# An attention and MLP kernel on one core: the value products of two half groups put into one run, numerators in two PSUM banks in turn, denominators in a projection bank, and the end of the program rearranged

## What is computed

```python
q = ((seq2 + b_self) @ Wq + bq)          # split into 16 heads of 32
k1 = ((x + b_prev) @ Wk + bk); k2 = ((seq2 + b_self) @ Wk + bk)
v1 = x @ Wv + bv;              v2 = seq2 @ Wv + bv
score = concat(where(mask, q @ k1.T, -inf), sum(q * k2)) * SCALE
w = softmax(score)
x = x + (w[:-1] @ v1 + w[-1] * v2) @ Wo + bo
h = gelu(x @ W1 + b1)                     # 2048 wide
x = x + concat(h @ W2 + b2, h @ We[e] + be[e])
```

## Time and profile before

| | us |
|---|---|
| median of 3 runs | 1795.75 (1795.39 to 1795.79) |
| profiled execution | 1807.21 |
| its span, first to last instruction | 1805.1 |
| PE busy | 1719.9 (95%) |
| mean granted PE clock | 0.976 |

### The profile page before, as it was taken

The page is one execution under the profiler, slowest core; times in us unless marked ns, Lnnn a source line. Parts: engine busy times, 40 slices in busy tenths (PEclk is TensorE's granted clock), DMA queues, the critical chain, the costliest instruction groups (busy, mean ns, idle before and its releaser), DMA issues.

```text
span 1805.1 us, 27962 instructions
## 1 busy us (share of the span) xinstructions
PE 1719.9 (95%) x8256; PEld 1262.1 (70%) x8256; DVE 942.4 (52%) x1430; ACT 709.5 (39%) x1259; POOL 663.4 (37%) x521
## 2 busy tenths in 40 slices
PE   6998999999999999999987899999999999999996
PEld 5765656666666666666652688888888888888885
DVE  4577576775866768757587643232232323232321
ACT  3253454444544445445344443323232323233222
POOL 3165577584874847748564301000010101010101
PEclk8999999999999999999996999999999999999998
DMA  6452444443534435244344342223131413232212
GB/s 143 76 114 51 91 103 107 86 97 73 120 90 91 96 85 119 69 103 87 80 110 121 109 122 50 68 48 86 46 87 41 87 52 75 61 66 72 47 30 53
DMA packets 370269, 149.45 MB, mean 83 GB/s; under 512 B 289226, under 2 KB 329162, under 8 KB 370194
## 3 DMA queue, kind: packets, MB, share of 16 engines
q1 hardware_dynamic: 364966, 146.28, 35.7%
q10 hardware_dynamic: 5228, 2.35, 0.5%
HBM read 70.41 MB, written 27.28 MB: 54 GB/s over the span
## 4 chain that ended last, share of the span: by engine, by line
PE 78%; issue 6%; DVE 5%; DMA 4%; SPq 3%; POOL 2%; ACT 1%; ACTq 0%; DVEq 0%; POOLq 0%
PE ps_proj L1258 14%; PE ps_max L1289 6%; PE ps_av L1210 6%; PE ps_av L1212 6%; PE ps_av L1211 6%; PE ps_av L1329 6%; PE ps_score L1316 5%; PE ps_proj L1210 3%; PE ps_proj L1211 3%; PE ps_proj L1212 3%; DMA stacks<-parts 3%; PE ps_score L1210 3%; PE ps_max L1212 3%; PE ps_score L1212 3%; PE ps_max L1210 3%
## 5 line engine op out<-in xcount | busy, mean ns | idle before, releaser
L729 ACT ACTIVATE p_f<-ps_score 128x512 f32<-128x512 f32 x512 | 303.8, 599 | 459.2 <-PE ps_score L1316 414.8
L941 DVE TENSOR_REDUCE m_col<-ps_max 128x1 f32<-128x512 f32 x512 | 328.7, 683 | 201.2 <-PE ps_max L1289 199.9
L604 POOL TENSOR_TENSOR p_sum<-p_sum,p_f 128x512 f32<-128x512 f32 x256 | 335.4, 1342 | 3.3 <-ACT p_f L729 3.3
L644 POOL TENSOR_TENSOR z_f<-z_f,a_raw 128x512 f32<-128x512 f32 x32 | 40.8, 1287 | 750.5 <-ACT z_f L842 730.0
L1135 DVE TENSOR_TENSOR h_lo<-h_f,h_hi 128x512 fp32r<-128x512 f32 x128 | 88.0, 687 | 412.2 <-ACT h_hi L833 412.1
L601 POOL TENSOR_TENSOR p_sum<-p_f 128x512 f32<-128x512 f32 x128 | 161.6, 1293 | 210.7 <-PE ps_av L1338 205.4
L1289 PE MATMUL ps_max<-stacks 97*128 97x512 f32 x512 | 189.3, 437 | 38.1 <-DVE m_col L941 19.4
L1258 PE MATMUL ps_proj<-in_hi,w_hi 128*128 128x512 f32 x512 | 207.8, 406 | 11.2 <-POOL in_lo L609 7.9
L1316 PE MATMUL ps_score<-stacks 99*128 99x512 f32 x512 | 209.0, 419 | 5.6 <-ACT p_f L729 5.4
L1210 PE MATMUL ps_av<-y_hi,w_hi 128*128 128x512 f32 x512 | 199.9, 390 | 6.6 <-ACT h_hi L833 3.8
L1258 PE MATMUL ps_proj<-in_lo,w_hi 128*128 128x512 f32 x512 | 205.6, 402 | 0.0
(11 more groups left out here) (122 smaller groups left out, 2729.1 us busy)
## 6 DMA issues: line engine op xcount, KB each, us to landing
stacks<-parts SPq DMA_DIRECT2D x384, 128.0 KB
raw<-in_x_dram SPq DMA_DIRECT2D x128, 64.0 KB, 2.3
raw<-in_fside_BxSxS_dram SPq DMA_DIRECT2D x128, 64.0 KB, 2.2
den<-own_scratch SPq DMA_DIRECT2D x128, 64.0 KB, 2.8
attn_scratch<-num SPq DMA_DIRECT2D x32, 256.0 KB, 3.0
x_raw<-in_x_dram SPq DMA_DIRECT2D x128, 64.0 KB, 2.2
we_raw<-in_L_cond_We_dram SPq DMA_DIRECT2D x32, 256.0 KB, 2.8
resid_scratch<-a_raw SPq DMA_DIRECT2D x32, 256.0 KB, 2.0
```

The costliest lines, as they stand in the source:

```text
L604: pool.tensor_tensor(p_sum[:, j], p_sum[:, j], now, ALU.add).then_inc(sum_made, 1)
L729: act.activation(p_f[:, i % FLIGHT], ps_score[i % 2][:, :], ACT.Exp, scale=SCALE).then_inc(p_made, 1)
L941: dve.tensor_reduce(m_col[:, n % C, n // C:n // C + 1], ps_max[n % 2][:, :], AX.X, ALU.max).then_inc(max_made, 1)
```

## The change

The batch's groups 1 to 3 do key tiles 2 and 3 of the group before in step 8, right ahead of tiles 0 and 1 of their own, so that 16 value products and 4 denominators stand in one run; group 0 keeps step 1. The numerators alternate between the two banks `ps_av`, the denominators go to `ps_proj[0]`, and DVE takes numerator and denominator together in step 10. The thirds of the projections are spread anew. In the last group the reciprocals and the normalization of the group before are put off until after the phase. In the MLP, `expert_high` of part 2 moves from slice 1 to slice 3 of the first batch. In the last batch the output products are reordered so that banks become complete one after the other, DVE adds bias and residual from PSUM and transposes, and SP and ACT store two quarters each; POOL, ACT and DRAM have no part in it.

```diff
@@ thirds_of
-            slots = ((4, 5, 5, 6, 7, 7, 9, 10, 11, 12, 13, 14), (0, 2, 3, 4, 5, 6, 9, 10, 11, 12, 13, 14),
-                     (0, 2, 3, 6, 7, 7, 9, 10, 11, 12, 13, 15), (0, 2, 3, 4, 5, 6, 9, 10, 11, 12, 13, 15))[g]
+            slots = ((4, 5, 5, 6, 7, 7, 9, 10, 12, 13, 14, 15), (0, 1, 3, 4, 6, 7, 9, 10, 12, 13, 14, 14),
+                     (0, 1, 3, 6, 7, 7, 9, 10, 12, 13, 14, 15), (0, 1, 3, 4, 6, 7, 9, 10, 12, 13, 14, 14))[g]
-        k_at, q_at = (6, 4, 4, 4), (8, 7, 8, 7)
+        k_at, q_at = (6, 4, 4, 4), (8, 8, 8, 8)
-        first_o = ps_proj + ps_max
+        first_o = (ps_proj[1], ps_max[0], ps_proj[0], ps_max[1])
-        ps_num, ps_den = ps_av
+        end_whole = (a_raw[:, 0], a_raw[:, 1], x_raw[:, :], x_t[:, :])
+        ps_den = ps_proj[0]
@@ ACT, rows
-                    if first and m < 2:
-                        expert_high(b, m + 1, True)
+                    if first and m in (0, 3):
+                        expert_high(b, 1 if m == 0 else 2, True)
@@ DVE, batch
-                        if i == 3 and started:
+                        if i == 10 and started:
                             numerator(*after(b, g, -1))
-                        if i == 10 and started:
                             denominator(*after(b, g, -1))
-                        if i in (13, 14) and started:
+                        if i in (13, 14) and started and not (last and g == C - 1):
-                        if i == 15 and started:
+                        if i == 15 and started and not (last and g == C - 1):
@@ DVE, new
+            def end_sum(c):
+                dve.wait_ge(end_mm, c + 1)
+                dve.wait_ge(whole_made, C * B)
+                if c == CS:
+                    dve.wait_ge(be_landed, DMA * B)
+                dve.scalar_tensor_tensor(out=end_z[:, c], in0=ps_out[c][:, :], scalar=bias_2[:, c:c + 1],
+                                         in1=end_whole[c], op0=ALU.add, op1=ALU.add).then_inc(end_made, 1)
+                dve.wait_ge(end_made, c + 1)
+                dve.transpose(end_z_t[:, c], end_z[:, c]).then_inc(z_t_made, 1)
@@ DVE, after the first phase
+            for n in range(4):
+                one_over_den(B - 1, C - 2, n)
+            normalize(B - 1, C - 2)
             hidden_low(0, 0)
@@ PE
                     if n == 2:
                         pe.wait_ge(q_hi_made, G + 1)
+                        wait(pe, den_made, G - 2)
-                    wait(pe, num_made, G)
+                    wait(pe, num_made, G - 1)
-                        if i == 1 and not (first and g == 0):
+                        if i == (8 if g else 1) and not (first and g == 0):
                             for t in (2, 3):
                                 value_burst(*after(b, g, -1), t)
                         if i == 8:
                             for t in (0, 1):
                                 value_burst(b, g, t)
                             if not (first and g == 0):
+                                if more:
+                                    pe.wait_ge(q_hi_made, C * b + g + 3)
+                                else:
+                                    pe.wait_ge(v2_made, C * B)
                                 denominators(*after(b, g, -1))
+            def end_outputs():
+                for m, c in ((KH - 2, 0), (KH - 2, 1), (KH - 1, 0), (KH - 1, 1),
+                             (KH - 2, 2), (KH - 1, 2), (KH - 2, 3), (KH - 1, 3)):
...
@@ SP and ACT, last batch
+            def end_result(c, quads):
+                sp.wait_ge(z_t_made, C * (B - 1) + c + 1)
+                for q in quads:
+                    sp.dma_start(blocks(out, B - 1, c, q),
+                                 end_z_t[QUAD * q:QUAD * (q + 1), c].rearrange("p (tb f) -> p tb f", f=QUAD)
+                                 ).then_inc(stored[c % 2], DMA)
```

More of the change, by code:

```diff
@@ L139, in cond_resid_program @@
         x_t = sb2("x_t", [P, S])
+        ending = two.enter_context(ExitStack())
+        end_z = ending.enter_context(nc.sbuf_tensor("end_z", [P, C, S], F32))
+        end_z_t = ending.enter_context(nc.sbuf_tensor("end_z_t", [P, C, S], F32))
+        ending.close()
         a_hi = sb2("a_hi", [P, C, S], F32R)
@@ L471, in batch @@
                         residual(0, 3)
-                    if not (first and g == 0):
+                    if not (first and g == 0) and not (last and g == C - 1):
                         store(*after(b, g, -1))
@@ L539, in rows @@
                     expert_weights(b, 3)
+                if last:
+                    for c in range(C):
+                        end_result(c, (0, 1))
+                    return
                 if not last:
@@ L646, in rows @@
             def rows(b, first, last):
-                for c in range(C):
+                for c in range(C if not last else 0):
                     add_residual(b, c)
@@ L878, in rows @@
                         y_high(b + 1, c)
-                for c in range(C if last else 2):
-                    result(b, c)
+                    for c in range(2):
+                        result(b, c)
+                else:
+                    for c in range(C):
+                        end_result(c, (2, 3))
             batches(act, rows)
@@ L1175, in rows @@
                         w2_low(w2_row[m])
-                    if first and m < 2:
-                        expert_low(b, m + 1)
+                    if first and m in (0, 3):
+                        expert_low(b, 1 if m == 0 else 2)
                     if m == (6 if first else 4):
@@ L1186, in rows @@
                     if 3 + C <= m < 3 + 2 * C:
-                        whole(b, m - 3 - C)
+                        if last:
+                            end_whole_of(m - 3 - C)
+                        else:
+                            whole(b, m - 3 - C)
                     if not last and m == KH - 4:
@@ L1200, in rows @@
                         y_low(b + 1, c)
-                for c in range(C if last else 2):
-                    turn_result(b, c)
+                for c in range(C):
+                    if last:
+                        end_sum(c)
+                    elif c < 2:
+                        turn_result(b, c)
             batches(dve, rows)
@@ L1448, in outputs @@
                 mm.then_inc(out_mm, 1)
+            def end_outputs():
+                for m, c in ((KH - 2, 0), (KH - 2, 1), (KH - 1, 0), (KH - 1, 1),
+                             (KH - 2, 2), (KH - 1, 2), (KH - 2, 3), (KH - 1, 3)):
+                    if c == 0:
+                        pe.wait_ge(h_lo_made, KH * (B - 1) + m + 1)
+                    at = slice(P * c, P * (c + 1))
+                    left = (w2_hi[:, m, at], w2_lo[:, m, at]) if c < CS else (we_hi[:, m], we_lo[:, m])
+                    mm = three(ps_out[c][:, :], left, (h_hi[:, m % 2], h_lo[:, m % 2]), False, m == KH - 1)
+                    if m == KH - 1:
+                        mm.then_inc(end_mm, 1)
             def rows(b, first, last):
@@ L1463, in rows @@
                         hidden(b, m + 2, range(C), first)
+                    if last and m == KH - 2:
+                        end_outputs()
+                        break
                     outputs(b, m, first)
```

25 lines of the change are left out of this document (19 added, 6 removed).

## The result

Measured: 1815.42 us (median of 6 runs, 1807.8 to 1837.05), against 1795.57 us before (6 runs, 1791.86 to 1796.51), ratio 1.0097 with a 95% interval of 1.0076 to 1.0119. Ratios leave out a run that lies more than 1.5% above the fastest of its kernel, here the one at 1837.05; the two medians by themselves give 1.011. The change makes the kernel 1% slower; 1787 was forecast, and 1813 was the end of the range. The profiled execution took 1808.08, its span 1806.0: 0.9 more than the *profiled* one of before, but 12.5 more than the median of before. It has 75% of the chain in place of 78%, DVE has 5% as before, and POOL has 5% for 2%, ACT 3% for 1% and "issue" 8% for 6%.

What follows compares the result with a forecast made beforehand. TensorE (PE), with 78% of the chain, was taken as the bound. Terms +19 +3 −15 −7 −8.5 gave −8.5 against the profiled 1807.21, carried over to the median 1795.75 as 1787; range 1760 to 1813.

Steps and rivals of the forecast that it cites:

- The long normalizations: First phase: the two normalize calls of about 9 us, behind POOL's unbroken additions, both go: −15 us.
- Rival C: In g = 1 normalize meets POOL's unbroken row in a new place, +7.4 each, +52: 1839; chance 0.10.
- Rival A: The two long normalizations are not there in the timed runs, or stay: slower, 1802; chance 0.25.
- Holes: Steps 2 and 5 of g = 1 to 3, left without filler, make PE wait for DVE's reductions: 0.9 to 1.0 each.
- The run itself: g = 1 to 3: one merged run of value products in place of two saves 0.31 each, 7 us over 24 merges.
- The waits for stacks: Group heads: later thirds cover the stacking DMAs, −0.9 for g = 3, −0.5 for g = 1, −0.7 for the other two.
- Steps 9 to 15: End of g = 3: PE still needs 7.30 from step 9 to the next group's start.
- g = 0 and g = 1: Group periods: g = 0 changes by −0.4, with +0.35 for denominators awaiting a projection bank; g = 1 by +0.44.
- The groups in sum: First phase: +2.46 for a batch, about +19 in all, and +3 for more clock falls in g = 2.
- The change of phase: Into the MLP: −2.1 from the put-off normalization and −5 from expert_high moved to slice 3, −7 together.
- The end: Last batch: banks done earlier, less DVE work and earlier stores, −8.5, bounds −6 and −10.
- The rival of free holes: Rival B: the new holes cost nothing since DVE catches up, so merges count −7 for +19: 1761; chance 0.15.

Runs made afterwards that it cites:

- the end alone: The kernel before with only the new end of the last batch (SP and ACT stores, DVE sum and transpose, output products reordered): 1787.91 us, ratio 0.9946.
- the wait on POOL: POOL waits for normalize to finish before a chosen addition of its row in each group; added to the changed kernel: 1819.07 us.
- expert_high: The kernel before with the new end, and expert_high and expert_low of part 2 moved from slice 1 to slice 3: 1784.64 us.
- later thirds: The kernel before with the new end, moved expert_high, and the last six thirds of g = 0, 2 and 3 later, no merge: 1777.31 us.
- the best order: No merge, new end, moved expert_high, thirds later in g = 0, 2, 3; with POOL's wait for normalize in those groups 1764.55 us, without it 1777.31.
- the two others: POOL's wait for normalize added to the changed kernel, 1819.07 us, and to the kernel before with new end and moved expert_high, 1786.2 us.

## Why the prediction was wrong, point by point

**The long normalizations: the step that failed.** "I take that it both go: −15", and then "I carry the difference over: 1787". In the profiled execution they went. But the timed runs of before had hardly any (the profile of the end alone, with none and the old groups, gives the median of before), so nothing could be gained there: the term is 0 in place of −15. The 11.5 by which the profiled execution lay above the median was already most of the price of those stalls; to start from the median and to take the 15 off as well counts it twice. "In a fixed order of instructions such a meeting repeats" is refuted: the same place has it in one run and not in the next. The changed groups can have them again, in a varying number. The ten profiles of kernels without the wait on POOL show 2 (before), 0 and 0 (end alone, expert_high) in the old order, 0, 0, 1, 3 and 4 with the changed groups, and 1 and 5 with later thirds. The ten hold 16 cases, the four with the wait none. The reason that I gave was the phase of the asking against POOL's beat. It does not decide: held off cases began 0.07, 0.41, 0.48, 0.74, 1.06 and 1.15 before the end of an addition, and for each of these the same phase passed normally in other batches. (Rival C's phase came: at the head of g = 2 DVE asks 1.15 before an addition ends, and is through after 1.71.) What selects one is open. What ends it is shown: in all 16 cases it ends 0.5 behind the last addition of POOL's unbroken row, and with POOL made to rest it doesn't occur. Rival A had the mechanism ("not there in the timed runs", 1802) and rival C the other half (it comes back, at +7.4 each), which I took as systematic at one place and not as chance at all of them; what happened is the two together. The port rule of the Trainium skill ("SBUF — State Buffer", section Who interferes with whom), a wait for one POOL instruction, holds for the median (1.1 after, 1.5 before) and fails for the long ones, where seven ends of POOL additions passed, in one case eight.

**Holes.** Forecast 0.9 to 1.0 each; measured 0.9 to 0.95 (two kernels). Right.

**The run itself.** Forecast −0.31; step 8 grew by 1.72 for a run that cost 2.05 apart. Right, and too small to pay for the hole. Net of one merge: +0.63 in g = 3.

**The waits for stacks.** Forecast −0.5 to −0.9, and they went, but in g = 2 DVE's normalize took their place: 0.83 and what follows in step 1. This had no effect, as POOL's last low part sets step 8 there: forecast 28.5, measured 28.50. That the number is met is luck in part: the last low part came 12.0 and not 12.5 after the head, so that step 8 began at +15.6 and not +16.0, and steps 9 to 15 took the 0.4 back.

**Steps 9 to 15: the term that was mis-sized.** The 13.45 up to step 8 of g = 3 is right to 0.15 (13.31). The 7.30 behind step 8, taken as unchanged, was too small in every group: 7.67 to 7.81, since the hole in step 11 uncovers ACT's two DMA issues. Moving that one third gives it back (25.82 for 26.17). 31 groups at 0.4 are 12 us.

**g = 0 and g = 1.** Forecast −0.4 and +0.44, measured +0.45 and +1.28: the step above, and in step 8 the projection bank: 0.75 in g = 0 (0.35 forecast) and 0.47 in g = 1, of which about 0.35 in each is in the small products.

**The groups in sum.** Forecast +19, and +3 for more falls of the clock. Against the profile of the end alone (888.49 from the first head to the last, no long normalization) the changed kernel has 913.32, +24.8. Six batches at +4.3 (0.45 + 1.28 + 1.6 + 0.97), +0.7 for the first and +2.3 for the last make +29, so the term of 19 was 10 too small, the 12 of steps 9 to 15 above all; the falls went the other way: in the six middle batches that profile has five, at 1.4 to 1.6 each, and one g = 2 that is 1.3 longer at full clock, this one has three falls: −4 and not +3.

**The change of phase.** Forecast −7, measured −4.1: −0.7 or −0.9 for the put-off work, −3.3 for expert_high. Of the wait of 3.75 in the earlier trace rows 0.96 is left (1041.00 below), and waits of 1.14 and 0.17 come at the first product of the MLP, now for y_lo, behind what was put off:

```profile
1021.68 0.47 PE L1262 MATMUL ps_av<-y_hi,w_hi 128*128 128x512 f32 x1 [1.14 <-DVE y_lo L1158]
1022.79 0.50 PE L1262 MATMUL ps_av<-y_hi,w_hi 128*128 128x512 f32 x1 [0.17 <-DVE y_lo L1158]
...
1041.00 0.47 PE L1262 MATMUL ps_av<-y_hi,w_hi 128*128 128x512 f32 x1 [0.96 <-ACT h_hi L851]
```

**The end.** Forecast −8.5, measured −7.1 and +0.4 in the last products, −8 by timed runs of the end alone. Right within 1.5.

Without the −15 the forecast's sum gives 1802. With the measured terms it is 1795.6 + 24.8 − 4.1 − 6.7 = 1809.6; the changed kernel's two lowest runs are 1808. What lifts its median to 1815 is not seen in its one profile and stays open. Falls of the clock are likely, since the same groups with the wait on POOL scatter as much and go with the clock; long normalizations are likely in the run at 1837, from the other kernels' profiles. The rival of free holes (1761) is refuted.

## What to carry to other kernels

Before a stall seen in a profile is entered as a gain, see whether the timed runs have it: if the profiled execution lies well above the median, its rare rows explain that difference first, and belong in the range and not in the sum. A step of filler that is taken out of PE's row must be laid against *every* engine that keeps step with PE (here DVE's 0.64 a tile, and ACT's 1 us of DMA issues between two exponentials), and the place for a hole is where none of them is behind: step 10 or 7 costs nothing, 1, 2, 5 or 11 costs 0.4 to 0.95. When a kernel's runs scatter by several times the size of one stall, one deliberate wait that keeps the two engines apart can be worth more than all reordering: 13 us here in the best order, and nothing in the two others to which it was added by itself.

## What the runs showed of the hardware

- A DVE tensor_tensor with both inputs and its output in SBUF normally waits for the POOL addition in progress (0.69 alone, 0.9 to 1.9 beside POOL). In some batches it is held off for 8.0 to 10.3 us (16 cases in ten profiles), until POOL's unbroken row of additions ends. The same request at the same phase passes in other batches and runs.
- POOL's addition during which such an instruction gets through takes 1.73 in place of 1.28.
- Two DMA issues by ACT between two exponentials leave it 1 us without work (0.99 in the changed kernel), which the profile doesn't count as busy.
- A run of products with 32 output partitions costs about 0.3 us beyond its products, in and out of it: 8 more products add 1.72 or 1.73 to a run that stands, and cost 2.05 by themselves.
- Products with few output partitions sometimes take longer than in an unbroken row: the eight small ones (x16) 0.9 for 0.55, four denominators (x8) 1.34 for 0.87. In the fast row of denominators four records start 0.007 apart and the next four 0.41 later; in the slow one each starts 0.08 to 0.14 behind the one before. Not explained.
- The granted clock fell in g = 2 of some batches: half of full speed for 3.4 us from about 12 us after the head (0.94 over the group), behind waits of 0.3 in steps 5 and 6 that the batches without a fall have too, and the group took 1.6 us longer. In the old order it fell in the same way in some g = 0, about 3 us after the head (38.2 for 36.6). Which batch has it differs between runs; what decides is open.
